# Moving the low part of w1's second half from GpSimd to VectorE

## What is computed

```python
q = layernorm(x) @ Wq.T + bq;  k = ctx @ Wk.T + bk;  v = ctx @ Wv.T + bv      # ctx: 4 x 154 rows of 256
scores = q @ k.T / sqrt(256), only the 32 largest of each row kept
x = x + tanh(g_xattn) * (softmax(scores) @ v @ Wo.T + bo)
h = relu(layernorm(x) @ W1 + b1)                                                # W1: 256 x 1024
x = x + tanh(g_ffn) * (h @ W2 + b2)
```

## Time and profile before

| | |
|---|---|
| median of 3 runs | 256.22 us (256.20 to 256.43) |
| the profiled execution | 256.42 us |
| its span | 254.6 us |
| PE busy | 249.3 us (98%) |
| DVE busy | 175.9 us (69%) |
| ACT busy | 155.1 us (61%) |
| POOL busy | 174.0 us (68%) |
| granted TensorE clock | full in all 40 slices |

### The profile page before, as it was taken

The page is one execution under the profiler, slowest core; times in us unless marked ns, Lnnn a source line. Parts: engine busy times, 40 slices in busy tenths (PEclk is TensorE's granted clock), DMA queues, the critical chain, the costliest instruction groups (busy, mean ns, idle before and its releaser), DMA issues.

```text
span 254.6 us, 6000 instructions
## 1 busy us (share of the span) xinstructions
PE 249.3 (98%) x2012; PEld 242.4 (95%) x2012; DVE 175.9 (69%) x743; ACT 155.1 (61%) x389; POOL 174.0 (68%) x267
## 2 busy tenths in 40 slices
PE   8999899999999999999999999999999999999995
PEld 7876699999999999999999999999999999999994
DVE  1699999978966767974699297966696287412042
ACT  2498676675665447665566547765656666655652
POOL 3479979997958884489548874589449954796300
PEclk9999999999999999999999999999999999999999
DMA  7992202101500320122110410101010011002011
GB/s 219 409 417 89 82 4 84 48 10 75 167 0 1 114 96 3 42 89 80 41 44 0 167 44 3 41 3 41 3 44 0 3 41 45 0 0 86 0 44 41
DMA packets 6878, 17.30 MB, mean 68 GB/s; under 512 B 800, under 2 KB 2368, under 8 KB 6592
## 3 DMA queue, kind: packets, MB, share of 16 engines
q1 hardware_dynamic: 6576, 16.77, 18.2%
q10 hardware_dynamic: 272, 0.16, 0.4%
HBM read 12.44 MB, written 4.19 MB: 65 GB/s over the span
## 4 chain that ended last, share of the span: by engine, by line
PE 85%; DMA 3%; POOL 3%; DVE 3%; ACT 3%; SPq 1%; issue 1%; DVEq 0%
PE y_ps L421 11%; PE y_ps L417 11%; PE y_ps L416 11%; PE z_ps L404 11%; PE z_ps L406 11%; PE z_ps L405 11%; PE sc_ps L337 5%; DMA w_in<-w 3%; PE pt_ps L356 3%; PE att_ps L375 1%; PE att_ps L374 1%; PE att_ps L372 1%; PE att_ps L373 1%; PE att_ps L386 1%; PE pt_ps L386 1%; DVE picked L962 1%
## 5 line engine op out<-in xcount | busy, mean ns | idle before, releaser
L1266 POOL TENSOR_TENSOR hid_lo<-hid,hid_hi 128x256 fp32r<-128x256 f32 x120 | 87.7, 744 | 45.8 <-ACT hid L742 45.4
L741 ACT ACTIVATE hid_hi<-z_ps,small_in 128x256 fp32r<-128x256 f32 x128 | 60.6, 473 | 61.8 <-PE z_ps L406 60.1
L404 PE MATMUL z_ps<-x2nt_hi,w_hi 128*128 128x256 f32 x256 | 73.1, 286 | 0.0
L406 PE MATMUL z_ps<-x2nt_hi,w_lo 128*128 128x256 f32 x256 | 71.5, 279 | 0.0
L405 PE MATMUL z_ps<-x2nt_lo,w_hi 128*128 128x256 f32 x256 | 71.0, 277 | 0.0
L416 PE MATMUL y_ps<-w_hi,hid_hi 128*128 128x256 f32 x248 | 65.7, 287 | 0.0
L417 PE MATMUL y_ps<-w_lo,hid_hi 128*128 128x256 f32 x248 | 64.4, 282 | 0.0
L742 ACT ACTIVATE hid<-z_ps,small_in 128x256 f32<-128x256 f32 x128 | 60.1, 470 | 0.0
L421 PE MATMUL y_ps<-w_hi,hid_lo 128*128 128x256 f32 x248 | 50.5, 282 | 0.0
L404 PEld LDWEIGHTS z_ps<-x2nt_hi,w_hi 128*128 128x128 f32 x256 | 48.2, 188 | 0.6 <-DVE x2nt_lo L996 0.6
L405 PEld LDWEIGHTS z_ps<-x2nt_lo,w_hi 128*128 128x128 f32 x256 | 48.2, 188 | 0.0
(11 more groups left out here) (148 smaller groups left out, 399.6 us busy)
## 6 DMA issues: line engine op xcount, KB each, us to landing
x_ring<-x SPq DMA_DIRECT2D x8, 512.0 KB, 5.1
out<-x SPq DMA_DIRECT2D x15, 256.0 KB, 2.0
xt_in<-x_t SPq DMA_DIRECT2D x7, 512.0 KB, 3.8
w_in<-w SPq DMA_DIRECT2D x2, 1024.0 KB, 10.3
wkq_in<-w_kq SPq DMA_DIRECT2D x1, 514.0 KB, 3.4
wvo_in<-w_vo SPq DMA_DIRECT2D x1, 513.0 KB, 6.5
xt_in<-x_t SPq DMA_DIRECT2D x2, 256.0 KB, 5.8
ctx_in<-ctx_t SPq DMA_DIRECT2D x1, 462.0 KB, 9.0
```

Source lines behind the costliest of these rows:

```text
L404: mm(dst, w1_hi[:, k, cols], hi[:, k, toks], start=k == 0, stop=False)
L406: last = mm(dst, w1_lo[:, k, cols], hi[:, k, toks], start=False, stop=k == KD - 1)
L741: func(hid_hi[:, c % RING, :], z_ps[c % 2][:, 0:2 * P], ACT.Relu, bias=b1[:, c:c + 1]).then_inc(hid_hi_made, 1)
L1266: nc.gpsimd.tensor_tensor(hid_lo[:, slot, :], hid[:, slot, :], hid_hi[:, slot, :], ALU.subtract).then_inc(hid_lo_made, 1)
```

## The change

POOL keeps only the first half of w1's low part. The second half is subtracted by DVE, between the statistics of the first pair (`residual(0, 0)`) and the second round of top-k of the second pair. It has a semaphore of its own, on which PE waits beside the old one.

```diff
+        second_w1_lo_made = sem("second_w1_lo_made")
@@ ffn_in, on PE
                 if u == 0 and c == 0:
-                    pe.wait_ge(w1_lo_made, KD)
+                    pe.wait_ge(w1_lo_made, 1)
+                    pe.wait_ge(second_w1_lo_made, 1)
                     pe.wait_ge(vals_copied, 4)
@@ on DVE
+            def second_w1_to_lo():
+                dve.wait_ge(w1_hi_made, 2)
+                nc.vector.tensor_tensor(w1_lo[:, 1, :], w1_in[:, 1, :], w1_hi[:, 1, :], ALU.subtract).then_inc(second_w1_lo_made, 1)
@@ the list of DVE
             residual(0, 0)
+            second_w1_to_lo()
             topk_round(0, 1, 1)
             normalise_second()
@@ on POOL
-            def w1_to_lo(k):
-                pool.wait_ge(w1_hi_made, k + 1)
-                nc.gpsimd.tensor_tensor(w1_lo[:, k, :], w1_in[:, k, :], w1_hi[:, k, :], ALU.subtract).then_inc(w1_lo_made, 1)
+            def w1_to_lo():
+
+                pool.wait_ge(w1_hi_made, 1)
+                nc.gpsimd.tensor_tensor(w1_lo[:, 0, :], w1_in[:, 0, :], w1_hi[:, 0, :], ALU.subtract).then_inc(w1_lo_made, 1)
@@ the list of POOL
-            w1_to_lo(0)
+            w1_to_lo()
             normalise_x2(0, 0)
-            w1_to_lo(1)
             w2_to_lo(0)
```

## The result

The changed kernel takes 256.98 us, median of 13 runs (256.85 to 257.12); the kernel before takes 256.38 over 13 runs of its own (256.20 to 256.49). The ratio is 1.0022, with a 95% interval of 1.0015 to 1.0029: 0.60 us slower, interval 0.39 to 0.74. The forecast was 256.55 with a term of +0.32; the time lies in the range of 256.2 to 257.2, and a little beyond the 0.2% that I had called "no difference".

What follows compares the result with a forecast made beforehand. PE was taken to bound the kernel, busy 249.3 of 254.6 us. DVE's longer queue and POOL's held-off norm, less the vanished wait for `picked`, gave +0.32 on the 256.22 median: 256.54, rounded to 256.55; range 256.2 to 257.2.

Steps and rivals of the forecast that it cites:

- DVE's instruction: DVE's new 1024-column subtraction at 24.20: 1.22 us long, 1.13 us of DVE's queue, bounds 0.6 and 1.3.
- POOL's norm held off by 0.84: POOL's first norm step (L1243, 24.45) waits for DVE's two-SBUF-input subtraction and ends 0.84 us later, as do both x2n.
- `ffn_in(0, 0)`: PE's first hidden product, behind x2nt_lo, starts at 29.59 instead of 28.80: +0.79 us.
- The wait for `picked` goes: PE's transposes of `picked` for the second pair start at 31.05 without waiting, against 30.59; second pick meets no POOL instruction.
- the transposes without a wait: Four PE transposes of `picked` take 0.36 us instead of 0.50, so `values_of(5)` starts at 31.41 against 31.09: +0.32.
- The upper bound: Start of `values_of(5)` on PE +0.46 us late, if POOL's norm is blocked until DVE's instruction ends (0.98 us).
- The added semaphore: PE's added wait on its own semaphore stands beside the old one and costs nothing; its DVE producer was done 4 us before.
- The lower bound: Start of `values_of(5)` on PE +0.24 us late, if POOL's small norm step is not blocked: 0.76 on DVE, nothing on POOL.
- The first rival: POOL's second w2 quarter holds DVE's second pick, `picked` is late: +1.0, 257.25; milder +0.55 to +0.8; chance 0.3 together.
- The second rival: DVE takes 1024 columns two per step, 0.6 us: -0.16, 256.05; chance 0.05, plus 0.1 with picks realigned.
- within 0.2%: Whole kernel's time changes by less than 0.51 us: chance 0.6, from forecast 0.45, unmoved case 0.1 and second rival 0.05.

Runs made afterwards that it cites:

- half move: Changed kernel with DVE subtracting only 512 of the 1024 columns and POOL the other 512 behind normalise_x2(0, 0); +0.57 us against the kernel before.
- removal alone: Kernel before without the low part of w1's second half on any engine, PE using the first half's instead; -0.46 us against before.
- runs fed from PSUM: Changed kernel, DVE's step replaced by two subtractions with one PSUM input into a spare tile: +1.13 us; with POOL also waiting for both x2n: +0.54 us.
- addition alone: Kernel before plus DVE's subtraction into a spare tile, POOL still making both halves and PE waiting for all; +0.91 us against before.
- third comparison: Timed runs of the changed kernel repeated without edit against the kernel before; +0.78 us.

## Why the prediction was right, and where it was off

Times are counted from the start of POOL's first w1 step, 21.98 before and 21.92 after.

*DVE's instruction*: 1.22 us predicted, 1.23 measured; its queue 1.13, measured 25.29 - 24.14 = 1.15. Right.

*POOL's norm held off by 0.84*: L1251 lasts 1.04, which is 0.85 more. The size was right. (The working has 1.09 us for the 1024 columns; at its own 1.04 ns a column they are 1.06, which gives 0.81.) The half move, with 0.32 more for 512 columns, bears the columns out: 0.53 us less for 512 fewer, 1.04 ns each. The rule of the Trainium skill that I had weighed ("SBUF — State Buffer", section "Who interferes with whom") gives the port to whoever comes first for its whole instruction. I had made 0.98 of it, and 0.85 was measured. The rows don't refute it, though: L1251 ends 0.05 us behind DVE's instruction, so it may have waited to that end with the first 0.14 of its own 0.19 us already past.

*`ffn_in(0, 0)`*: 7.65 behind the yardstick's start in place of 6.82, +0.83; predicted +0.79. I had derived it from x2nt_lo behind DVE's queue, and had not listed the third wait of this product, for ACT's copy of `values_of(3)`. Both chains are late by the same amount, x2nt_lo by 0.85 and ACT's copy by 0.85, so the number came out though one of the two was missing. That they agree is no accident: DVE's x2n of tile 1 started at 26.39, as soon as the held-off norm was there (L1254 of POOL, 25.65 + 0.70 = 26.35), so this norm stands in front of both.

*The wait for `picked` goes*: it does, and the second pick lasts 0.31. The transposes are +0.53 late, against +0.46 predicted: 0.04 is carried over from `ffn_in`, and the twelve matmuls took 1.49 us from the first of them to the transposes, not 1.46.

*The term that was mis-sized* is the last one, the transposes without a wait. I priced the step from them to the next group at 0.36 us, from a place where a hidden product follows them. Here `values_of(5)` follows, and the step is 31.49 - 31.06 = 0.43 (0.44 in the run with the removal alone). So 0.07 of the 0.14 that I let come back there did not. Together, 0.04 + 0.03 + 0.07 = 0.14 makes the difference between +0.32 and +0.46. The upper bound was +0.46 as well, but for a norm held off by 0.98 us; that the measured stretch meets it is chance.

*The added semaphore* was put at nothing. At its wait it cost nothing that shows in the changed kernel; in the tail the traces have +0.12 us with it, a term that was in no part of the sum. With it the sum is 0.46 + 0.12 = 0.58.

*The lower bound was wrong in its mechanism.* "No blocking of POOL" was to give +0.24. The runs fed from PSUM show that without the block POOL's w2 step gets ahead of DVE's x2n and the time rises by 1.13 us; only with a wait that keeps them apart is it +0.29 in the stretch. I had looked for two-input instructions when I asked who could be held off, and DVE's x2n is not one.

*The first rival* (POOL's second w2 step in the way of the second pick) is what the half move shows: a pick of 1.40 us and a wait at the transposes, though at +0.45 in the stretch and not +1.0, as x2n was late by only 0.33 us there. In the addition alone the pick lasts 1.41 us too, but behind POOL's first w2 step, which POOL's w1 step had kept late. Neither is what the change does. *The second rival* falls by the 1.23 us of the row; the Trainium skill's "VectorE: DVE Perf Modes", section "The perf-mode tier table", agrees with it: no faster mode for two fp32 tensors.

*The chances.* I gave 0.6 to "within 0.2%" and 0.3 to slower. The stretch says +0.46 us, which would be within; with the tail it is about +0.58, and the timed runs say +0.60, both just beyond. With a term of +0.32 to +0.46 and a bound at 0.51 the two cases were nearer to each other than 0.6 to 0.3. The 0.12 us of the tail bring the traces to within 0.03 us of two of the three timed comparisons. What stays open is what the additional semaphore does at the end, and the remaining 0.2 us of the third comparison (+0.78). The latter could be scatter of the first 22 us: w1_hi started anywhere from 12.48 to 13.04 us in the traces, at 12.48, 12.61 and 12.77 in the three of the changed kernel and at 12.66 in that of before, so the traces show no late start that belongs to the changed kernel.

## What to carry to other kernels

Before work is moved between VectorE and GpSimd, lay the two timelines side by side and mark which instructions would run at once: here one POOL step of 1.3 us in front of a 0.3 us pick cost 0.4 us of a PE-bound kernel, nearly what the whole move cost on balance. A step whose result is needed only later can still be on the path, through what it holds off or pushes behind it; take it out for one run to see its worth. And then look for the order that keeps the two engines' steps apart (a split step, a wait) before moving work to an engine whose queue stands in front of the critical one. List every semaphore that the critical instruction waits for: two chains that end together hide each other. Compare the ends of two traces too, and not only the stretch that was changed.

## What the runs showed of the hardware

- A one-input fp32 instruction of VectorE (TENSOR_SCALAR, 128x256, SBUF to SBUF, two per-partition scalars in SBUF) is held off by a running GpSimd step like a two-input one: 1.30 us beside a w2 step that began 0.13 us earlier, 0.40 where that step waited. It also holds GpSimd off: POOL's x2n beside it lasts 0.68 us, and 0.55 in the run where DVE's x2n comes later.
- The same length of work with one input in PSUM did not hold off POOL's norm step: that lasted 0.19 us beside it, and 1.04 beside the instruction with both inputs in SBUF.
- In one trace a GpSimd step that waited behind one such VectorE instruction did not get in when the next followed at once: x2n on POOL lasted 1.74 us behind a 256-column and a 1024-column instruction of DVE.
- The delay of a blocked GpSimd step goes by the blocker's columns: POOL's two-column step, arriving 0.24 us behind DVE's instruction, was late by 0.85 us with 1024 columns and by 0.32 us with 512, 1.04 ns a column.
- With one semaphore more in the program the execution went on 4.58 to 4.63 us behind the start of DVE's last instruction (nine traces), without it 4.46 to 4.49 (four traces).
